# Layers 0 and 1 with images held as 4 rows x 32 channels, and three of four sign pieces on GpSimd

## The chip, the cores and the metric

The kernel runs on one core of one Trainium2 chip. A core has five engines that run side by side: TensorE (PE, matmuls and transposes), VectorE (DVE), ScalarE (ACT), GpSimd (POOL) and SyncE (SP, which issues DMAs); ACT issues DMAs too. The metric is device time in microseconds (us). A conclusion needs the profile for where the time goes and the timed runs for how much it is.

## The reference

An input x of 16 images, 224 x 224 pixels, 32 channels, float32, NHWC, passes four residual layers. Each starts with a group normalization of its input (16 groups of 2 channels over a whole image).

```
x = x + L0(gn(x))   # mean over the image -> W, b -> clip(0, 28) -> int dy, dx; the image shifted by (dy, dx), zeros outside
x = x + L1(gn(x))   # sign(gn(x)) convolved 3x3 ('SAME') with the sum of 4 sign weights, plus a bias
x = x + L2(gn(x))   # relu( spectral part + x @ W.T + b )
x = x + L3(gn(x))   # the same with other weights
# spectral part: DCT along columns (32 modes kept), real FFT along rows (32 modes kept),
# a 32 x 32 complex channel mix for each of the 32 x 32 modes, and both transforms back
```

Layer 1 needs only the sign of the normalized image, that is, each value compared with a threshold (m1 in the code), and layer 2 needs the mean and variance of each output image of layer 1 and its 32 x 32 modes.

## The kernel before

It runs five phases one after the other, with a barrier between them. In the names of tensors the first letters tell the phase.

1. Layers 0 and 1 for all images (A_, shift_conv_forward). It writes the output x2s, and for layer 2 the spectrum spec of every image and its mean and variance (statm).
2. The channel mix of layer 2 (MB_, mix_modes).
3. The rest of layer 2 (B_, third_layer): inverse transforms, the 1x1 product, relu, the sum, the forward transform for layer 3. It reads x2s and writes x3s.
4. The channel mix of layer 3 (MC_).
5. The rest of layer 3 (C_, last_layer).

**Layers 0 and 1.** An image in SBUF is a tile of 128 partitions: 4 neighbouring columns x 32 channels; the free dimension runs over the 56 groups of four columns and the 224 rows. Two images are in work at a time, in two buffers. Body(b) of every engine does, interleaved, the convolution of image b, the shift of image b + 1 and the loading of image b + 2, in 9 slots (s = 0 to 8). The tiles of x, 112 rows x 1024 values, arrive by SP's DMAs in the order of use. TensorE transposes each into PSUM (L373, four transposes to a unit of 448 columns, 28 units an image), once for the image as it is (A_aps, copied to the image by ACT with a sum, L525, and squared for the variance, L536), and once for the image shifted by (dy, dx), which is loaded again from other addresses (A_sps, masked where it is outside and added to the image by VectorE, L738 to L749). VectorE makes the signs in four pieces of 14 column groups (L773 to L781): one compare to bf16, a full copy, and two copies of 32 partitions, so that there are two sign tensors (signa, signb). With these the 3x3 convolution of a unit of 448 columns is 6 matmuls of 128 rows x 64 columns of the array (L415), in pairs that use its two halves. VectorE adds the result to the image (L755). ACT squares it (L577). TensorE transposes the result back (L426), ACT copies it (L547) and stores it to x2s in NHWC order; the same copies are the input of the forward row transform (L440, ACT L560). The column transform of an image (the function spectrum: turn_spec L452, ACT's copy L568 into one of two colpart buffers, forward_cols L461) is done in eight rounds during slots 0 and 1 of the next body. Statistics of an image are a chain of short instructions that goes VectorE, TensorE, VectorE, ACT, VectorE, TensorE, VectorE (L683 to L728); between images the order is: last shifted unit, center, centered (L761 to L767, the threshold m1), signs, statistics.

**Layer 2 (third_layer).** An image is 4 rows x 32 channels: partition 32 i + c holds channel c of the rows 4 l + i, l = 0 to 55. Since x2s is NHWC, each image is loaded in eight chunks of eight DMAs (L1168) and turned by 16 VectorE transposes of 32 x 32 blocks (turn_in, L1347). Then, for 14 units (e) of 896 columns: TensorE's 1x1 product (L1253) and inverse column transform (L1263), VectorE's relu and sum (L1377), ACT's squares (L1307) and store. The forward transform of image b - 1 stands between them: VectorE transposes it (turn_out, L1370), TensorE transforms (L1225, L1235), VectorE turns the results (L1357, L1364). The image is loaded and turned in units e = 6 to 13 of the image before; TensorE waits at the start of an image until all 16 transposes are done.

The order of all work is written out by hand in these bodies; loops over images repeat them. Each engine executes its instructions strictly in order, and all else is semaphores.

## Time and profile before

| | us |
|---|---|
| median of 3 timed runs | 3808.79 (3801.92 to 3814.15) |
| the profiled execution's own time | 3800.75 |
| its span, first to last instruction | 3798.7 |
| layers 0 and 1 (first convolution added at 172.1, last at 1792.1) | about 0 to 1816 |
| channel mix of layer 2 | about 1819 to 1950 |
| layer 2 (first product at 1991.8, last transposes at 3070.2) | about 1951 to 3090 |
| channel mix of layer 3 and layer 3 | about 3090 to 3798.7 |

| engine | busy us | share of the span |
|---|---|---|
| PE | 2990.2 | 79% |
| PE weight loads | 1622.4 | 43% |
| DVE | 2738.1 | 72% |
| ACT | 1522.8 | 40% |
| POOL | 36.9 | 1% |

Busy shares are means over phases with different limits, so they are read by phase. A matmul's end is modelled, so what a group of matmuls costs is read from the distance between starts. The granted clock is the TensorE clock in parts of 2.4 GHz.

### The profile page before, as it was taken

What the parts mean: (1) busy time and instruction counts of PE and PEld (TensorE: products, weight loads), DVE (VectorE), ACT (ScalarE), POOL (GpSimd) and SP (SyncE); (2) the same over time, 40 slices, a digit from 0 to 9 for tenths busy, and PEclk for the clock granted to TensorE, in tenths of its full rate; (3) what the DMA queues carried; (4) which work ended last, traced back from release to release, by engine and by line L of the source; (5) the groups of instructions that cost most, each with busy time, mean ns of one, the idle gap of its engine ahead of it and who ended that gap; (6) DMA issues with size and microseconds to landing.
All of it is one profiled execution on the core that took longest, in us unless ns stands there. A gap on an engine that the chain in (4) does not pass through costs nothing. (4 is left out here: it accounts for less than half of the span.)

```text
span 3798.7 us, 64095 instructions
## 1 busy us (share of the span) xinstructions
PE 2990.2 (79%) x20528; PEld 1622.4 (43%) x20528; DVE 2738.1 (72%) x4615; ACT 1522.8 (40%) x3060; POOL 36.9 (1%) x23
## 2 busy tenths in 40 slices
PE   2688888888888888888348787887878735999997
PEld 2455555555554555544243333333333315444443
DVE  2566666666566666665537889989898744899998
ACT  3477766666677766655312222222222213000000
POOL 0000000000000000000100000000000010000000
PEclk9799998999899998989658899898898965999998
DMA  4566765666666675653657757767576353999998
GB/s 121 160 196 191 207 203 169 183 177 187 173 194 177 199 207 169 184 163 110 137 150 222 234 196 224 219 213 226 191 243 192 141 120 103 345 387 386 383 386 296
DMA packets 244496, 793.86 MB, mean 209 GB/s; under 512 B 41706, under 2 KB 76190, under 8 KB 233396
## 3 DMA queue, kind: packets, MB, share of 16 engines
q1 hardware_dynamic: 172692, 473.01, 42.4%
q10 hardware_dynamic: 70912, 316.72, 23.7%
q8 instruction: 143, 2.34, 0.3%
q14 instruction: 141, 1.16, 0.1%
q0 software_dynamic: 608, 0.63, 0.1%
HBM read 464.31 MB, written 329.10 MB: 209 GB/s over the span
## 5 line engine op out<-in xcount | busy, mean ns | idle before, releaser
L1307 ACT ACTIVATE B_junk<-B_im,B_nk 128x896 bf16<-128x896 f32 x224 | 233.4, 1042 | 855.9 <-DVE B_im L1377 659.0
L1253 PE MATMUL B_ring<-B_im,B_wnorm 128*128 128x448 f32 x896 | 413.3, 605 | 157.7 <-DVE B_im L1347 155.9
L755 DVE SCALAR_TENSOR_TENSOR A_image<-A_cps,A_cbias,A_image 128x448 f32<-128x448 f32 x448 | 303.3, 681 | 226.8 <-PE A_cps L415 200.8
L1576 PE MATMUL C_ring<-C_im,C_wnorm 128*128 128x448 f32 x896 | 387.8, 571 | 24.4 <-DVE C_ubuf L1633 19.0
L415 PE MATMUL A_cps<-A_signa,A_cwa 128*64 128x448 bf16 x1344 | 354.1, 378 | 63.9 <-DVE A_signa L781 43.0
L373 PE MATMUL A_aps<-a_k_ident,A_tin 112*128 112x112 f32 x1792 | 274.8, 297 | 108.2 <-ACT A_image L525 72.3
L415 PE MATMUL A_cps<-A_signb,A_cwb 128*64 128x448 bf16 x1344 | 354.8, 378 | 0.0
L547 ACT ACTIVATE A_tout<-A_aps 112x512 f32<-112x512 f32 x448 | 242.4, 591 | 266.4 <-PE A_aps L426 266.1
L1253 PEld LDWEIGHTS B_ring<-B_im,B_wnorm 128*128 128x128 f32 x896 | 172.9, 204 | 402.7 <-issue 334.5
L1225 PE MATMUL B_ring<-B_rout,iB_k_rowf 128*64 128x512 f32 x896 | 269.3, 684 | 76.4 <-DVE B_rout L1370 76.1
L749 DVE SCALAR_TENSOR_TENSOR A_image<-A_sps,A_lin,A_image 128x448 f32<-128x448 f32 x448 | 304.4, 682 | 13.4 <-PE A_sps L373 3.2
L525 ACT ACTIVATE A_image<-A_aps 128x448 f32<-128x448 f32 x448 | 240.3, 541 | 166.3 <-PE A_aps L373 161.9
L373 PE MATMUL A_sps<-a_k_ident,A_tin 112*128 112x112 f32 x1792 | 275.7, 280 | 39.6 <-DVE A_image L749 19.8
L1377 DVE SCALAR_TENSOR_TENSOR B_im<-B_ring,B_im 128x896 f32<-128x896 f32 x224 | 239.5, 1071 | 82.1 <-PE B_ring L1263 80.1
L1347 DVE STREAM_TRANSPOSE B_im<-B_rin 128x896 f32<-128x896 f32 x256 | 284.1, 1110 | 14.8 <-DMA B_rin<-x2s 10.3
L373 PEld LDWEIGHTS A_aps<-a_k_ident,A_tin 112*128 112x128 f32 x1792 | 205.2, 158 | 177.0 <-ACT A_image L525 71.0
L373 PEld LDWEIGHTS A_sps<-a_k_ident,A_tin 112*128 112x128 f32 x1792 | 184.1, 146 | 200.1 <-issue 148.5
L1642 DVE STREAM_TRANSPOSE C_rout<-C_im 128x2048 f32<-128x2048 f32 (+1 forms) x128 | 259.4, 2028 | 5.9 <-DMA out<-C_rout 4.0
L1370 DVE STREAM_TRANSPOSE B_rout<-B_im 128x2048 f32<-128x2048 f32 (+1 forms) x128 | 256.3, 2023 | 0.0
L426 PE MATMUL A_aps<-a_k_ident,A_image 128*112 128x128 f32 x1792 | 240.9, 278 | 18.1 <-ACT A_tout L547 18.1
L1576 PEld LDWEIGHTS C_ring<-C_im,C_wnorm 128*128 128x128 f32 x896 | 159.1, 189 | 216.2 <-issue 163.1
L1648 DVE SCALAR_TENSOR_TENSOR C_im<-C_ring,C_im 128x896 f32<-128x896 f32 x224 | 234.9, 1069 | 14.7 <-PE C_ring L1586 12.7
(195 smaller groups left out, 4023.9 us busy)
## 6 DMA issues: line engine op xcount, KB each, us to landing
A_tin<-in_x SPq DMA_DIRECT2D x441, 448.0 KB, 4.9
B_rin<-x2s SPq DMA_DIRECT2D x1024, 112.0 KB, 3.4
x2s<-A_tout ACTq DMA_DIRECT2D x224, 448.0 KB, 4.4
x3s<-B_im ACTq DMA_DIRECT2D x112, 896.0 KB, 5.0
C_im<-x3s SPq DMA_DIRECT2D x112, 896.0 KB, 13.0
out<-C_rout ACTq DMA_DIRECT2D x192, 256.0 KB
out<-C_rout ACTq DMA_DIRECT2D x192, 192.0 KB
out<-C_rout ACTq DMA_DIRECT2D x64, 128.0 KB
```

Of the source, the lines that this page charges most:

```text
L373: last = nc.tensor.transpose(dst[:, j * HR:(j + 1) * HR], src[:, (4 * s + j) * P:(4 * s + j + 1) * P], con["k_ident"][0:HR, 0:HR])
L415: last = nc.tensor.matmul(cps[n % 2][64 * g:64 * g + 64, 0:2 * SIZE], wts[:, tap, :], src[:, j0:j0 + 2, 1 + tap:1 + tap + SIZE], start=(ta ...
L426: last = nc.tensor.transpose(aps[v % 2][0:HR, j * P:(j + 1) * P], image[par][:, j0 + j, half * HR:(half + 1) * HR], con["k_ident"][:])
L547: nc.scalar.activation(tout[u % OUTS][:, v % 2, :], aps[v % 2][0:HR, :], ACT.Copy).then_inc(a_copied, 1)
L749: nc.vector.scalar_tensor_tensor(out=dst, in0=t[:, :, :], scalar=lin[par][:, 0:1], in1=dst, op0=ALU.mult, op1=ALU.add, accum_out=addsum[:, ...
L755: nc.vector.scalar_tensor_tensor(out=dst, in0=cps[n % 2][:, 0:2 * SIZE].rearrange("p (j r) -> p j r", r=SIZE), scalar=cbias[par][:], in1=d ...
L1225: last = nc.tensor.matmul(bank[64 * side:64 * side + 64, hq, :], con["k_rowf"][:, t, :], rout[p % 2][:, t, q0:q0 + BANK], start=(t == 0), ...
L1253: nc.tensor.matmul(slot(par, ("add", e))[:, lane % 2, 0:2 * SIZE], wnorm[par][:], im[par][:, EVN * e:EVN * (e + 1)].rearrange("p (m s) -> ...
L1347: nc.vector.transpose(turned_view(im[par], j0, ch * CHQ, CHQ), flat_view(rin[slot][:, t, :])).then_inc(turned_in, 1)
L1370: nc.vector.transpose(flat_view(rout[p % 2][:, t, 0:wide * C]), turned_view(im[par], j0, p * PAIRQ, wide)).then_inc(rout_full, 1)
L1576: nc.tensor.matmul(slot(add_place(e))[:, lane % 2, 0:2 * SIZE], wnorm[par][:], im[par][:, EVN * e:EVN * (e + 1)].rearrange("p (m s) -> p s ...
L1642: nc.vector.transpose(flat_view(rout[p][:, 0:wide * C]), turned_view(im[par], SECOND * t, p * PIECEQ, wide)).then_inc(rout_full, 1)
```

## The change

Layers 0 and 1 get the layout that layer 2 has: 4 rows x 32 channels. From this follow all other parts.

- **Loading.** x comes in 16 tiles of 28 columns (CHQ) an image, four DMAs of 32 partitions each, and again for the shifted image. TensorE no longer transposes them: VectorE does, with 32 x 32 block transposes, straight into the image (turn_x), or into a tile `moved` that it masks and adds (add_shifted). Three image buffers take the place of two. ACT sums and squares the tiles from SBUF (x_tile).
- **Bodies of 16 slots** with 14 convolution units of 896 columns; two tables, X_BY and S_BY, say how many tiles of either kind are done by the end of each slot.
- **Convolution.** For each unit, 6 matmuls of the whole 128 x 128 array (rows inside the groups of four) and 12 of 32 x 32 (from the neighbouring group, with every second element read and written), in place of 2 x 6 matmuls of 128 x 64 in the kernel before.
- **Signs.** A single sign form, no shifted copies. Piece 0 (8 row pairs of 448 values) is made by VectorE; pieces 1, 2 and 3 (9, 9 and 8 of 448) by GpSimd, into two buffers used in turn: piece 1 as soon as piece 0 is done, piece 2 after 4 units of the convolution, piece 3 after 7.
- **Forward transform.** Columns first, then rows. The first part has half the matmuls (L507); the second has, in each of eight rounds, a copy into one colpart buffer (before: two) and four matmuls of 128 columns with 64 x 64 weights.
- **Outputs.** x2s is stored straight from the image, in the image's own layout. The spectrum is stored in 8 DMAs whose runs in DRAM are 32 values (before: one DMA with rows of 512 values).
- **Layer 2** loads x2s in 7 DMAs an image into the image buffer; its rin buffers, chunks and turn_in are gone. It loads image b + 1 when image b - 1 has been turned out, squared and stored.

The mixes and layer 3 are unchanged.

```diff
-        image = [sb(f"image{i}", [P, NBLK, SIZE]) for i in range(2)]
-        signa = sb("signa", [P, NBLK * RP], bf16)
-        signb = sb("signb", [P, NBLK * RP], bf16)
-        tin = [sb(f"tin{i}", [HR, TW]) for i in range(RING)]
+        image = [sb(f"image{i}", [P, NPIX]) for i in range(3)]
+        sign = [sb(f"sign{i}", [P, (CHL + 2) * LPW + 8], bf16) for i in range(2)]
+        rin = [sb(f"rin{i}", [P, CHQ * C]) for i in range(RING)]
+        moved = sb("moved", [P, TN])
...
-        colpart = [sb(f"colpart{i}", [HR, BANK]) for i in range(2)]
+        colpart = sb("colpart", [64, BANK])
...
+        X_BY = [0, 2, 5, 7, 9, 11, 13, 14, 15, 16, 16, 16, 16, 16, 16, 16]
+        S_BY = [0, 0, 0, 1, 2, 3, 4, 6, 8, 10, 13, 16, 16, 16, 16, 16]
...
             def store_spec(b):
                 sp.wait_ge(spec_sb, b + 1)
-                sp.dma_start(spec[bass.ds(b, 1)].rearrange("o p m -> (o p) m"), specout).then_inc(spec_stored, 16)
...
+                planes = plane.rearrange("(g e c) (m y) -> g e m c y", g=4, e=2, m=16)
+                for e in range(2):
+                    for g in range(4):
+                        sp.dma_start(planes[g, e],
+                                     specout[64 * e + 16 * g:64 * e + 16 * g + 16, :].rearrange("m (c y) -> m c y", y=MODES)
+                                     ).then_inc(spec_stored, 16)
...
             def conv(b, n):
...
-                for tap in range(3):
-                    for g, (src, wts) in enumerate(((sa, cwa), (sbb, cwb))):
-                        last = nc.tensor.matmul(cps[n % 2][64 * g:64 * g + 64, 0:2 * SIZE], wts[:, tap, :],
-                                                src[:, j0:j0 + 2, 1 + tap:1 + tap + SIZE],
-                                                start=(tap == 0), stop=(tap == 2), skip_group_check=True)
...
+                def edges(u_top, u_bottom):
+                    for tap in range(3):
+                        nc.tensor.matmul(banks[bottom, u_top, 0:LPN].rearrange("p (j s) -> p s j", s=2), cedge[top, tap, :],
+                                         above(2 * n + u_top, tap), start=False, stop=False, skip_group_check=True)
+                        nc.tensor.matmul(banks[top, u_bottom, 0:LPN].rearrange("p (j s) -> p s j", s=2), cedge[bottom, tap, :],
+                                         below(2 * n + u_bottom, tap), start=False, stop=False,
+                                         skip_group_check=True)
...
+                whole(0, 0)
+                whole(1, 0)
+                edges(0, 1)
+                whole(0, 1)
+                whole(1, 1)
+                edges(1, 0)
+                whole(0, 2)
+                whole(1, 2).then_inc(conv_full, 1)
...
+            def add_shifted(b, q, k, at_tile):
...
+                nc.vector.transpose(moved[:, :].rearrange("p (l q s) -> p q l s", q=CHQ, s=2),
+                                    flat_view(rin[at_tile % RING][:, :])).then_inc(tile_turned, 1)
...
+                nc.vector.scalar_tensor_tensor(out=dst, in0=m[:, lo:16, :], scalar=lin[:, 0:1], in1=dst, op0=ALU.mult,
+                                               op1=ALU.add, accum_out=addsum[:, k:k + 1]).then_inc(shift_added, 1)
...
         @block.gpsimd
...
+            def signs(b, q, c):
+                if c == 1:
+                    pool.wait_ge(sign_full, b + 1)
+                    if not isinstance(b, int) or b > 0:
+                        pool.wait_ge(conv_full, UNITS * b)
+                else:
+                    pool.wait_ge(conv_full, UNITS * b + (4 if c == 2 else CHL))
...
+                nc.gpsimd.tensor_scalar(rows[:, lo - CHL * c + 1:hi - CHL * c + 1, 2:2 + LPN], lps(q)[:, lo:hi, :], m1[:], 2.0,
+                                        ALU.is_ge, ALU.mult).then_inc(sign_rest, 1)
...
# third_layer
-            def turn_in(b, par, ch):
...
+            def load(b, par, k):
+                cols = slice(2 * EVN * k, 2 * EVN * (k + 1))
+                sp.dma_start(im[par][:, cols], src[bass.ds(b, 1)].rearrange("o p m -> (o p) m")[:, cols]).then_inc(in_full[par][k], 16)
```

**The order on VectorE inside an image.** Before, in the middle of a body: A_cps holds convolution units of 448 columns, A_sps shifted units; REGISTER_ALU rows count the loop's semaphores.

```order
L753 REGISTER_ALU
L755 SCALAR_TENSOR_TENSOR A_image0,A_convsum0<-A_cps0,A_cbias0,A_image0 128x448 [waits A_conv_full]
L733 REGISTER_ALU
L738 SCALAR_TENSOR_TENSOR A_sps0<-A_sps0,A_nmean1,A_rmask1 128x4x28 [waits A_shift_full]
L644 REGISTER_ALU
L749 SCALAR_TENSOR_TENSOR A_image1,A_addsum<-A_sps0,A_lin1,A_image1 128x4x112 [waits A_step]
```

The changed kernel at the like place (slot 5 of a body):

```order
L826 SCALAR_TENSOR_TENSOR A_image1,A_convsum1<-A_cps1,A_cbias1,A_image1 128x896 [waits A_conv_full]
L886 REGISTER_ALU
L795 STREAM_TRANSPOSE A_image0<-A_rin1 128x28x16x2 [waits A_in_full1,A_junk_done]
L803 REGISTER_ALU
L805 STREAM_TRANSPOSE A_moved<-A_rin2 128x28x16x2 [waits A_in_full2,A_shift_added]
L807 REGISTER_ALU
L817 SCALAR_TENSOR_TENSOR A_moved<-A_moved,A_nmean,A_rmask 128x224 [waits A_tile_turned]
L704 REGISTER_ALU
L820 SCALAR_TENSOR_TENSOR A_image2,A_addsum<-A_moved,A_lin,A_image2 128x16x56 [waits A_step]
```

A unit has twice the columns; the transposes are VectorE's, and the sum of the shifted tile reads two operands from SBUF (moved and the image), where it read one from PSUM (A_sps).

**The order on TensorE at the start of a body**, between two convolution units, where the second part of the transform of the image before stands. Before:

```order
L461 MATMUL A_vps<-A_colpart0,a_k_dctf 32x64 [waits A_a_copied]
L461 MATMUL A_vps<-A_colpart0,a_k_dctf 32x64 x7
L452 MATMUL A_aps0<-a_k_ident,A_rowspec 112x128 [waits A_a_copied]
L452 MATMUL A_aps0<-a_k_ident,A_rowspec 112x128 x3
```

The changed kernel, the end of four rounds and the convolution unit 1 behind them:

```order
L524 REGISTER_ALU
L529 MATMUL A_vps<-A_colpart,a_k_fwdr 64x128 [waits A_a_copied]
L529 MATMUL A_vps<-A_colpart,a_k_fwdr 64x128 x3
L524 REGISTER_ALU
L529 MATMUL A_vps<-A_colpart,a_k_fwdr 64x128 [waits A_a_copied]
L529 MATMUL A_vps<-A_colpart,a_k_fwdr 64x128 x3
L466 MATMUL A_cps1<-A_sign0,A_cfull 128x448 [waits A_conv_added,A_sign_full]
L466 MATMUL A_cps1<-A_sign0,A_cfull 128x448
```

A round's matmuls read the one buffer colpart, which ACT may fill again only when they are done; VectorE's convolution unit 1 stands behind four such rounds, unit 2 behind four more.

**GpSimd's queue in the loop**, empty before:

```order
L934 ISA [waits A_sign_full]
L944 TENSOR_SCALAR A_sign<-A_image,A_m 128x9x448 [waits A_conv_full]
L936 REGISTER_ALU
L944 TENSOR_SCALAR A_sign<-A_image,A_m 128x9x448 [waits A_conv_full]
L936 REGISTER_ALU
L941 MEMSET A_sign 128x448 [waits A_conv_full]
L942 ISA
L944 TENSOR_SCALAR A_sign<-A_image,A_m 128x8x448 [waits A_pool_step]
```

The three compares of an image, each 3584 or 4032 values to a partition.

## Rows read from the trace of the kernel before

**Rows 1.** Windows: span of layers 0 and 1, and one image of layer 2.

```profile
core 0: us, PE busy (x) PEld busy (x) DVE busy (x) ACT busy (x) POOL busy (x), PEclk, DMA share, GB/s
172.10:1792.10 1620.00, 1379.43 (x11115) 838.74 (x11116) 1059.69 (x2894) 1094.32 (x2336) 0.00 (x0) 0.92 0.62 181
2307.50:2374.70 67.20, 54.85 (x248) 21.92 (x248) 59.62 (x68) 15.89 (x28) 0.00 (x0) 0.88 0.64 203
```

**Rows 2.** One line: threshold of each image (ns min/median/max, first to last start).

```profile
L766 DVE COPY A_m<-A_mps x16: 157/159/160, 162.7 to 1730.9; 128x1 f32<-128x1 f32 x16
```

**Rows 3.** One line: after unit 0 of each image in layer 2.

```profile
L1382 DVE TENSOR_SCALAR B_nk<-B_sums x16: 153/154/155, 1999.7 to 2982.9; 128x1 f32<-128x1 f32 x16
```

**Rows 4.** Waits, 300 to 1700 us: total us, times, longest.

```profile
DVE A_image L755 <- PE A_cps L415: 167.1, 59, 5.7
```

**Rows 5.** Timeline of DVE, layers 0 and 1 (start us, us, instruction).

```profile
97.83 0.18 DVE L684 TENSOR_REDUCE A_sm<-A_xsum 128x1 f32<-128x28 f32 x1 [37.07 <-ACT A_xjunk L536]
...
105.46 0.22 DVE L728 TENSOR_SCALAR A_cmask<-a_k_cols,A_sm 128x7 f32<-128x7 f32 x1
...
640.38 0.68 DVE L749 SCALAR_TENSOR_TENSOR A_image<-A_sps,A_lin,A_image 128x448 f32<-128x448 f32 x1
...
641.00 0.68 DVE L755 SCALAR_TENSOR_TENSOR A_image<-A_cps,A_cbias,A_image 128x448 f32<-128x448 f32 x1
```

**Rows 6.** Timeline of PE, layers 0 and 1, with two convolution pairs.

```profile
599.32 0.58 PE L415 MATMUL A_cps<-A_signa,A_cwa 128*64 128x448 bf16 x1
...
635.86 0.35 PE L415 MATMUL A_cps<-A_signa,A_cwa 128*64 128x448 bf16 x1
...
636.05 0.35 PE L415 MATMUL A_cps<-A_signa,A_cwa 128*64 128x448 bf16 x1
...
638.00 1.04 PE L426 MATMUL A_aps<-a_k_ident,A_image 128*112 128x128 f32 x8
...
645.47 1.94 PE L440 MATMUL A_vps<-A_tout,a_k_fwd 112*64 112x512 f32 x8
```

**Rows 7.** Timeline of ACT: a copy of the second transform, a square.

```profile
609.41 0.60 ACT L568 ACTIVATE A_colpart<-A_aps 112x512 f32<-112x512 f32 x1 [0.38 <-PE A_aps L452]
...
623.86 1.03 ACT L577 ACTIVATE A_junk<-A_image,A_nk 128x896 bf16<-128x896 f32 x1
```

**Rows 8.** Groups by line (busy us, mean ns): VectorE's compare.

```profile
L773 DVE TENSOR_SCALAR A_signa<-A_image,A_m 128x3136 bf16<-128x3136 f32 x64 | 118.3, 1848 | 0.5
```

**Rows 9.** One line: GpSimd's long instruction, a memset.

```profile
L929 POOL MEMSET MB_moving<- x1: 6915/6915/6915, 1832.2 to 1832.2; 64x8192 f32 x1
```

**Rows 10.** SP's issues: a plain one, and one of 1024 runs of 512 bytes.

```profile
3.58 0.43 SPq L126 DMA_DIRECT2D a_k_rows<-k_rows  x1
...
1850.30 2.72 SPq L911 DMA_DIRECT2D MB_wmode<-in_L_conv_R_real  x1
```

**Rows 11.** DMA issues: count, KB each, median us to landing.

```profile
B_rin<-x2s SPq DMA_DIRECT2D x1024, 112.0 KB, 3.4
```

**Rows 12.** Timeline of DVE in one image of layer 2.

```profile
2309.05 4.45 DVE L1370 STREAM_TRANSPOSE B_rout<-B_im 128x2048 f32<-128x2048 f32 x2
...
2343.47 1.09 DVE L1377 SCALAR_TENSOR_TENSOR B_im<-B_ring,B_im 128x896 f32<-128x896 f32 x1 [2.29 <-PE B_ring L1263]
...
2344.68 2.25 DVE L1347 STREAM_TRANSPOSE B_im<-B_rin 128x896 f32<-128x896 f32 x2
2346.86 1.05 DVE L1377 SCALAR_TENSOR_TENSOR B_im<-B_ring,B_im 128x896 f32<-128x896 f32 x1
```

**Rows 13.** Timeline of PE in the same image.

```profile
2307.50 4.99 PE L1253 MATMUL B_ring<-B_im,B_wnorm 128*128 128x448 f32 x8 [8.22 <-DVE B_im L1347]
...
2332.84 6.27 PE L1225 MATMUL B_ring<-B_rout,iB_k_rowf 128*64 128x512 f32 x16 [3.41 <-DVE B_rout L1370]
...
2343.36 3.65 PE L1225 MATMUL B_ring<-B_rout,iB_k_rowf 128*64 128x512 f32 x8
...
2351.96 3.80 PE L1235 MATMUL B_ring<-B_gbuf,iB_k_colf 128*64 128x512 f32 x16 [0.64 <-DVE B_gbuf L1357]
2355.70 3.41 PE L1253 MATMUL B_ring<-B_im,B_wnorm 128*128 128x448 f32 x8
...
2360.01 1.13 PE L1214 MATMUL B_ring<-B_vbuf,iB_k_invs 64*128 64x512 f32 x4
```

More of the change, by code:

```diff
@@ L229, in shift_conv_forward @@
         spec_stored = sem("spec_stored")
-        stored = [sem(f"stored{i}") for i in range(OUTS)]
+        stored = [sem(f"stored{i}") for i in range(3)]
         mean_in = sem("mean_in")
@@ L506, in _ @@
[L506 to L513 removed]
+                    if has_s and s == 12:
+                        statistics(b, 4)
```

925 lines of the change are left out of this document (468 added, 457 removed).

## The prediction

> **What bounds the kernel now.** I read the windows of the two changed phases first [rows 1]: in layers 0 and 1 TensorE is busy 85% of the time at a granted clock of 0.92, VectorE 65%, ScalarE 68%, GpSimd nothing; in the image of layer 2 VectorE has 89%, TensorE 82%. The threshold comes every (1730.9 - 162.7)/15 = 104.5 us [rows 2], layer 2's first unit every 65.5 us [rows 3]. In the waits, VectorE's convolution sum waits for TensorE 167 us over 59 times [rows 4]: layers 0 and 1 are bound by TensorE, with VectorE in its shadow in most places. In layer 2 the two go in lockstep in the first half of an image, and TensorE starts the image 8.22 us late behind VectorE's transposes of the input [rows 13].
>
> **The change, layers 0 and 1, per image.** TensorE loses all transposes of the input, so VectorE becomes the long engine. Its costs: a transpose of 896 values 1.09 us (two starts 2.18 us apart), a sum of 896 about 1.0 [rows 12]; a sum of 672 values by the same rate 0.8.
>
> - Slots 2 to 11: 10 convolution sums x 1.0, 14 transposes of x tiles x 1.09 = 15.3, 16 of shifted tiles = 17.4, the sums of the shifted tiles 8 x 1.0 + 8 x 0.8 = 14.4, masks 4.8 (one of 896, one of 672 and nine of 224 values, each with a wait for its own end: 1.0 + 0.8 + 9 x 0.33), the image's statistics 1.9 (nine tiny instructions, by the chain in [rows 5]). Together 63.8 us, VectorE without a pause. TensorE has here per slot a convolution unit, one transposing back and half a column transform. A pair of two concurrent half-array matmuls starts 0.19 us after the one before, eight transposes take 1.04 us [rows 6]. With the twelve 32 x 32 matmuls in pairs, a unit is 6 x 0.19 + 6 x 0.19 + 0.2 = 2.5 us, a slot 4.1: hidden behind VectorE's 6.4.
> - Seam, slots 12 to 15, where VectorE waits for TensorE in turn: sum 12 1.0, center 0.3, TensorE's average and unit 13 (behind GpSimd's last piece) 3.4, sum 13 1.0, centered 0.3, sign piece 0 2.6 (3584 values by the compare's 1848 ns for 3136 = 2.1 [rows 8], and a memset), then the chain of statistics 105.46 + 0.22 - 97.83 = 7.85 [rows 5] and 1.6 for its two more mask copies and its hops behind TensorE's queue. 18.1 us.
> - Start of a body, convolution 0's end to sum 2. Before, eight rounds used two colpart buffers; now one. A round is ScalarE's copy 0.6 [rows 7], four matmuls, and two hops of 0.2, one after the other. The matmuls of 128 columns cost between 0.52 (at the 0.13 of a transpose) and 1.04 (twice it, since a chain that starts anew each time is short and alone); I take 1.04, so 2.04 a round, and with the first four transposes 0.5 four rounds are 8.7. So 8.7 + unit 1 2.5 + turn back 1.1 + 8.7 + unit 2 2.5 + 0.2 = 23.7 us, in which VectorE has little to do.
> - Sum 105.6, and 2 for a half clock after TensorE's waits (a convolution matmul is 0.58 us at half clock against 0.35 [rows 6]): 107.5 us.
>
> ScalarE loses the copies of the transposed x, gains squares from SBUF (896 values, 1.03 us [rows 7]); I get 79 us an image, 38 of them in slots 2 to 6 beside VectorE's 37: close, not bounding.
>
> **GpSimd's pieces.** The trace of before has no compare on it, only a memset: 6915 ns for 8192 values [rows 9]. At that rate a piece of 4032 values is 3.4 us; two such passes (one read, one write) 6.8, three 10.2. I take 6. Piece 1 runs beside the chain of statistics, piece 2 from unit 4, piece 3 from unit 7. If nothing on VectorE is held, they cost nothing: the convolution that needs one comes several slots later. VectorE's new work, though, is made of instructions with two operands in SBUF (the shifted sums read moved and the image). If those stand still while a piece runs, each piece costs its length less the 1.5 to 2 us that an instruction in flight or of another kind covers: 3 x 4 = 12 us an image. Bounds 0 and 26 (three times 10.2 - 1.7). No row of before has GpSimd and VectorE together, so this is the term with the widest bounds. I take 12, in between, because all of VectorE's long instructions in slots 4 to 8 are transposes and such sums, and VectorE is the long engine there.
>
> By the Trainium skill, "SBUF — State Buffer", section "Who interferes with whom", a VectorE instruction with two inputs in SBUF and a GpSimd instruction that reads SBUF take turns for a whole instruction; by "GPSIMD Engine Reference", section "Performance versus the Vector engine", simple arithmetic there is about half VectorE's rate or less, an estimate of 6.0 to 8.7 us a piece. No row here shows either. By the one rule alone the period is some 12 to 20 us longer than without it; a page that lets one-input compares run near line rate would leave 3.4 us, and 5 us an image.
>
> **The spectrum's store** was one DMA with long rows. Now it is eight with 4096 runs of 128 bytes. An issue of 1024 runs costs SP 2.72 us, a plain one 0.43 [rows 10], so 4 x 2.72 = 11 us of SP's queue in slot 4, where the tiles' loads stand behind it. Four tiles in the ring cover about 8 us; a tile behind them takes its own four issues and a landing like 3.4 us [rows 11]. A stall of 0 to 9 us, I take 4, near the middle since cover and queue are about equal.
>
> **Sum of the phase.** 107.5 + 12 + 4 = 123.5 against 104.5: +19.0, x 15 = +285. Last image (no shifted work, but TensorE alone in its slots and both halves of the spectrum at the end) +18. Start: two fewer big memsets and copies, fewer transposes in the first image, -12.
>
> **Layer 2.** An image was 65.5 us. Its first half, 2309.05 (first turning out) to 2343.47 (the sum behind a wait of 2.29) = 34.4 us, alternates turning out 4.45 us for two, TensorE's rows 6.27, products [rows 12, 13]: unchanged. The second half, 31.1 us, held the 16 transposes of input, 17.4 us of VectorE. Without them TensorE sets it: rows 3.65, a step of products 2360.01 - 2355.70 = 4.31, columns 3.80, 4.31, small inverse 1.06 to 1.13, 4.31 = 21.4, and the sum ahead with its hop 1.3. Period 57.1. The input now comes into the image buffer itself after image b - 1 is turned out and stored, some 26 us ahead of its use; 6.4 MB at the 181 to 203 GB/s of the windows [rows 1] take 32 to 35 us, but the first of seven parts about 5, and the parts are used one after the other. I add 2 for this and the clock: 59, -6.5 x 15 = -97. The start of the phase loses an image's chunks and 16 transposes before the first product, -25. Together -122; bounds -40 (the second half still lockstep, the load late) and -230 (the 8.22 and 3.41 waits go too).
>
> **Total.** 285 + 18 - 12 - 122 = +169 on the profiled execution's 3800.75 (span 3798.7), 3970; the median shown is 8 above that execution, so 3978, rounded to 3975.
>
> **Rivals.**
> A, the other side: the pieces hold nothing and the store is hidden. Period 107.5, 45 + 18 - 12 - 122 = -71: 3737. The sign turns where the period is 104.5 + 116/15 = 112.2, that is where GpSimd and store together cost under 4.7 us an image. For it: the pieces start several slots early, GpSimd was idle [rows 1], the ring has cover. Against: VectorE has no slack left in slots 2 to 11.
> B, slow pieces: 10.2 us each and held all the while, 25.5 instead of 12, so a period of 137: 15 x 32.5 - 116 = +371, 4180. For it only the count of passes; against it, the memset's 0.84 ns a value [rows 9].
> C, the 32 x 32 matmuls don't run in pairs: a unit is 18 x 0.19 + 0.2 = 3.6, 1.1 more. In slots 2 to 11 that stays hidden (5.2 of 6.4 us), but units 1, 2, 12 and 13 stand on the path: +4.4, period 128, 15 x 23.5 - 116 = +236, 4045. For it: they read and write every second element, a thing that no row shows.
> By the Trainium skill, "DMA: Bandwidth & Descriptors", section "Specifications", pieces under 512 bytes miss the line rate, so the runs of 128 bytes would also land late; no row here shows such a run, and only the next image's last turn waits for it.
>
> **Chances.** The forecast 0.44, A 0.28, B 0.14, C 0.14. B's upper part alone is outside 3730 to 4150. Within 0.3% (11 us, what a measurement can tell) 0.05, between A and the forecast; faster 0.27, slower 0.68. If A or its neighbours hold, the faster end lies near 3730; both signs have weight, so the forecast's own range stands beside: 3880 to 4070.
>
> **What would show it.** Right: the period of the threshold (L837 of the changed kernel) about 123; L944 at about 6 us; shifted sums (L820) much longer than 1.0 us, or the instruction before them stretched, exactly beside a piece; transposes (L795, L805) 1.1; TensorE idle in slots 2 to 11; rounds of the second transform (L520, L626, L529) 2.05 apart; VectorE waiting in slot 4 or 5 for rin with SP's queue in L367; layer 2's period 57 to 59. Wrong: L820 at 1.0 beside L944 (A); L944 over 9 us (B); the starts of L471 and L473 0.19 apart singly, not in pairs (C); a convolution that waits for GpSimd's piece itself; a layer 2 still at 65.

## The result: 19% slower, and the profile after

The changed kernel takes 4538.23 us (median of 4 runs, 4516.48 to 4568.82), the kernel before 3805.36 (4 runs): a ratio of 1.193 (95% interval 1.186 to 1.201). 3975 was predicted and 4180 for the worst rival. The direction was right, the size was not: +733 us for +170.

The profiled execution took 4568.82 us, the longest of the four, with a span of 4567.0; before it was 3798.7, so 768 us are to be found in the profile. Two lines give their places, the threshold of each image and the first unit of each image of layer 2, as in [rows 2, 3] (ns min/median/max, first to last start):

```profile
L837 DVE TENSOR_SCALAR A_m<-A_mps x16: 152/154/158, 166.0 to 2550.4; 128x1 f32<-128x1 f32 x16
...
L1461 DVE TENSOR_SCALAR B_nk<-B_sums x16: 153/154/155, 2849.1 to 3744.4; 128x1 f32<-128x1 f32 x16
```

| | before | after | difference, us |
|---|---|---|---|
| up to the first threshold | 162.7 | 166.0 | +3 |
| 15 images of layers 0 and 1 | 15 x 104.5 | 15 x 159.0 | +816 |
| last threshold to layer 2's first unit | 268.8 | 298.7 | +30 |
| 15 images of layer 2 | 15 x 65.5 | 15 x 59.7 | -88 |
| the rest | 815.8 | 822.6 | +7 |

Layer 2 did what was said of it (59 predicted, 59.7 measured). Nearly all of the loss is in the period of layers 0 and 1: 159.0 us, where 123.5 was expected. It is a mean of fifteen intervals; the first is 132.3 us, the last 150.0, and those between are 157 to 164.

What GpSimd's line says is already outside every bound of the prediction. Below it stand GpSimd's timeline and VectorE's in one image, with piece 1 of the next image at the end (start us, us, instruction):

```profile
L944 POOL TENSOR_SCALAR A_sign<-A_image,A_m x48: 12344/13838/13840, 169.2 to 2620.7; 128x4032 bf16<-128x4032 f32 x32, 128x3584 bf16<-128x3584 f32 x16
```

```profile
1336.81 13.84 POOL L944 TENSOR_SCALAR A_sign<-A_image,A_m 128x4032 bf16<-128x4032 f32 x1 [53.03 <-PE A_cps L466]
...
1365.31 12.35 POOL L944 TENSOR_SCALAR A_sign<-A_image,A_m 128x3584 bf16<-128x3584 f32 x1 [0.20 <-POOL A_sign L941]
1434.12 13.84 POOL L944 TENSOR_SCALAR A_sign<-A_image,A_m 128x4032 bf16<-128x4032 f32 x1 [56.47 <-DVE A_sign L844]
```

```profile
1298.89 1.15 DVE L826 SCALAR_TENSOR_TENSOR A_image<-A_cps,A_cbias,A_image 128x896 f32<-128x896 f32 x1 [7.25 <-PE A_cps L466]
...
1318.26 1.15 DVE L826 SCALAR_TENSOR_TENSOR A_image<-A_cps,A_cbias,A_image 128x896 f32<-128x896 f32 x1 [18.21 <-PE A_cps L466]
...
1331.96 1.15 DVE L826 SCALAR_TENSOR_TENSOR A_image<-A_cps,A_cbias,A_image 128x896 f32<-128x896 f32 x1 [10.52 <-PE A_cps L466]
...
1338.73 9.50 DVE L857 TENSOR_TENSOR A_sm<-A_sm 128x1 f32<-128x1 f32 x1
...
1369.94 6.64 DVE L817 SCALAR_TENSOR_TENSOR A_moved<-A_moved,A_nmean,A_rmask 128x224 f32<-128x224 f32 x1
...
1429.82 1.15 DVE L826 SCALAR_TENSOR_TENSOR A_image<-A_cps,A_cbias,A_image 128x896 f32<-128x896 f32 x1 [7.92 <-PE A_cps L466]
...
1434.47 11.07 DVE L747 TENSOR_TENSOR A_sm<-A_sm 128x1 f32<-128x1 f32 x1
```

A multiplication of one value to a partition (L747) takes 11.07 us; alone it takes 0.16. A masking (L817) of 0.45 us takes 6.64. These three begin while a piece of GpSimd runs, and what they take beyond their own time is 10.9 + 9.3 + 6.2 = 26.4 us in this image. The same lines are held in nearly every image, L817 by 4.7 to 9.4 us. The transposes of 896 values in the same stretches keep their 1.1 us. The four convolution sums (L826) show another thing: VectorE stands 7.25, 18.21, 10.52 and 7.92 us for units 0, 1, 2 and 13 of TensorE.

TensorE shows why. Its timeline at the start of that body, first after the stall of the chain, then 20 us later, and at the end unit 0 of the next body:

```profile
1281.67 0.59 PE L424 MATMUL A_mps<-A_mv,a_k_pair 128*128 128x1 f32 x2 [11.87 <-DVEq L750]
...
1293.02 1.02 PE L471 MATMUL A_cps<-A_sign,A_cedge 32*32 32x448 bf16 x1
...
1293.76 1.02 PE L471 MATMUL A_cps<-A_sign,A_cedge 32*32 32x448 bf16 x1
...
1298.64 1.92 PE L520 MATMUL A_aps<-a_k_ident,A_rowspec 128*64 128x128 f32 x8
...
1310.88 0.93 PE L466 MATMUL A_cps<-A_sign,A_cfull 128*128 128x448 bf16 x2
...
1318.02 1.71 PE L493 MATMUL A_aps<-a_k_ident,A_image 128*112 128x128 f32 x8
...
1327.94 0.55 PE L466 MATMUL A_cps<-A_sign,A_cfull 128*128 128x448 bf16 x2
...
1328.77 0.57 PE L471 MATMUL A_cps<-A_sign,A_cedge 32*32 32x448 bf16 x1
...
1329.15 0.57 PE L471 MATMUL A_cps<-A_sign,A_cedge 32*32 32x448 bf16 x1
...
1331.76 1.04 PE L493 MATMUL A_aps<-a_k_ident,A_image 128*112 128x128 f32 x8
...
1453.04 0.55 PE L466 MATMUL A_cps<-A_sign,A_cfull 128*128 128x448 bf16 x2
...
1456.86 1.04 PE L520 MATMUL A_aps<-a_k_ident,A_rowspec 128*64 128x128 f32 x8
```

A convolution unit is 1331.76 - 1327.94 = 3.8 us at full clock and 7.1 at half clock (1310.88 to 1318.02), four rounds of the second transform 8.0 and 12.2. An edge matmul starts 0.38 us after the one before it on its side at full clock, 0.74 at half. A pair of 128 x 64 matmuls of as many columns took 0.19 [rows 6]. The L473 matmuls stand beside the L471 ones within 0.01 us, so they do run in pairs: the pair itself is slow.

The windows give the granted clock (PEclk), 0.92 before [rows 1]. The stretches are many images, the start of the body, slots 2 to 11, the seam's wait for unit 13, and the chain of statistics:

```profile
core 0: us, PE busy (x) PEld busy (x) DVE busy (x) ACT busy (x) POOL busy (x), PEclk, DMA share, GB/s
400.00:2400.00 2000.00, 1531.30 (x6496) 589.42 (x6498) 1318.04 (x1798) 889.31 (x1687) 494.22 (x49) 0.74 0.45 135
...
1299.60:1332.00 32.40, 29.91 (x140) 16.80 (x139) 3.67 (x7) 8.99 (x16) 0.00 (x0) 0.69 0.10 29
1332.00:1421.70 89.70, 68.54 (x308) 23.91 (x306) 82.27 (x102) 54.14 (x107) 26.66 (x3) 0.81 0.71 209
1421.70:1433.70 12.00, 11.69 (x36) 3.00 (x36) 3.97 (x9) 0.21 (x1) 0.00 (x0) 0.57 0.27 78
1433.70:1447.00 13.30, 1.26 (x8) 1.15 (x7) 12.00 (x8) 2.38 (x5) 12.88 (x1) 0.69 0.00 0
```

In every one of these stalls of some 12 us the clock falls to half while TensorE idles; when it comes back differs. In the body shown it is at half clock, but for 3.4 us before unit 0, until about 1319. Behind the next stall, of 12.04 us, unit 0 runs at full clock (1453.04 to 1456.86, 3.8 us), as it does in 5 of the 14 bodies between the first and the last; from the end of the chain to sum 2 these take 33.5 us, the others 37.7 to 40.5 (35.7 once). Unit 13 runs at half clock in all 14.

### The profile page after: what moved, and what is told of

It is laid out like the page before. It is cut to its first block and busy times, and to the rows that moved or that the text cites. A ratio compares the mean times of both kernels' runs of the same rounds, so it can differ in the third digit from the quotient of the medians.

```text
span 4567.0 us, 58488 instructions
## 1 busy us (share of the span) xinstructions
PE 3492.9 (76%) x17264; PEld 1475.1 (32%) x17264; DVE 3045.1 (67%) x3640; ACT 1493.5 (33%) x2708; POOL 684.9 (15%) x87
## 5 line engine op out<-in xcount | busy, mean ns | idle before, releaser
L944 POOL TENSOR_SCALAR A_sign<-A_image,A_m 128x4032 bf16<-128x4032 f32 (+1 forms) x48 | 640.3, 13340 | 1770.6 <-DVE A_sign L844 993.1
L471 PE MATMUL A_cps<-A_sign,A_cedge 32*32 32x448 bf16 x1344 | 737.5, 695 | 0.0
L473 PE MATMUL A_cps<-A_sign,A_cedge 32*32 32x448 bf16 x1344 | 737.3, 695 | 0.0
L826 DVE SCALAR_TENSOR_TENSOR A_image<-A_cps,A_cbias,A_image 128x896 f32<-128x896 f32 x224 | 257.2, 1149 | 698.0 <-PE A_cps L466 698.0
L466 PE MATMUL A_cps<-A_sign,A_cfull 128*128 128x448 bf16 x1344 | 454.0, 427 | 8.1 <-issue 8.1
L507 PE MATMUL A_vps<-A_tout,a_k_dctj 112*32 112x512 f32 x896 | 294.4, 792 | 133.5 <-ACT A_tout L606 133.2
L493 PEld LDWEIGHTS A_aps<-a_k_ident,A_image 128*112 128x112 f32 x1792 | 279.7, 196 | 241.8 <-issue 196.4
L795 DVE STREAM_TRANSPOSE A_image<-A_rin 128x896 f32<-128x896 f32 x256 | 274.5, 1097 | 84.3 <-DMA A_rin<-in_x 83.3
L805 DVE STREAM_TRANSPOSE A_moved<-A_rin 128x896 f32<-128x896 f32 x256 | 281.4, 1099 | 34.5 <-DMA A_rin<-in_x 25.6
L820 DVE SCALAR_TENSOR_TENSOR A_image<-A_moved,A_lin,A_image 128x896 f32<-128x896 f32 (+1 forms) x256 | 265.0, 1035 | 9.1
L590 ACT ACTIVATE A_junk<-A_image,A_nx 128x896 bf16<-128x896 f32 (+1 forms) x256 | 242.9, 949 | 8.5
## 6 DMA issues: line engine op xcount, KB each, us to landing
C_im<-x3s SPq DMA_DIRECT2D x112, 896.0 KB, 12.2
```

The costliest lines, as they stand in the source:

```text
L466: return nc.tensor.matmul(banks[:, u, 0:LPN], cfull[:, tap, :], straight(2 * n + u, tap), start=(tap == 0), stop=(tap == 2), skip_group_ch ...
L471: nc.tensor.matmul(banks[bottom, u_top, 0:LPN].rearrange("p (j s) -> p s j", s=2), cedge[top, tap, :], above(2 * n + u_top, tap), start=Fa ...
L473: nc.tensor.matmul(banks[top, u_bottom, 0:LPN].rearrange("p (j s) -> p s j", s=2), cedge[bottom, tap, :], below(2 * n + u_bottom, tap), st ...
L493: last = nc.tensor.transpose(aps[half][0:HR, l * P:(l + 1) * P], image[q][:, first:first + 2 * HR].rearrange("p (j s) -> p s j", s=2)[:, l ...
L507: last = nc.tensor.matmul(vps[32 * g:32 * g + 32, :], con["k_dctj"][:, half, :], tout[G % OUTS][:, half, :], start=(half == 0), stop=(half ...
L795: nc.vector.transpose(turned_view(image[q], SECOND * t, ch * CHQ, CHQ), flat_view(rin[slot][:, :])).then_inc(tile_turned, 1)
```

## Experiments

Three questions: is it GpSimd's piece that holds VectorE, and by what rule; why is the edge pair twice as slow; and what is left when both are gone. Ratios are to the kernel before, 95% intervals in brackets. "Period" is that of the threshold in layers 0 and 1, (last start - first start)/15.

### All four sign pieces on VectorE

```diff
+                    if has_v and s == 0:
+                        more_signs(q, 1)
                     if has_v and s < UNITS:
                         add_conv(b, q, s)
+                    if has_v and s in (3, 6):
+                        more_signs(q, 2 if s == 3 else 3)
...
# GpSimd
-                for c in (1, 2, 3):
-                    signs(b, q, c)
```

> All four sign pieces on VectorE: piece 1 ahead of convolution sum 0, pieces 2 and 3 behind sums 3 and 6. Theory (GpSimd's compare holds VectorE's instructions with two operands in SBUF): the holds of 10.9 us (L747), 9.3 us (L857) and 6.2 us (L817) an image go, three compares of about 2.3 us come, of which the first lies where VectorE waits for TensorE; net 26.4 - 4.6 = 22 us an image, 15 x 22 = 330, and some more where TensorE's half clock came from its waits for held instructions: period of the threshold 159 to about 130 to 137, time 4140 to 4230. Rival (the time is TensorE's: the 32x32 matmuls and the half clock, and the held instructions stand where VectorE would have waited anyway): the period stays above 150, time above 4400.

4202.6 us, 1.105 (1.102 to 1.108); period (2210.1 - 166.1)/15 = 136.3. The main theory's number. L747 takes 0.16 us again. The compares of 4032 values came out dearer than expected, two thirds of the 48:

```profile
L852 DVE TENSOR_SCALAR A_sign<-A_image,A_m x48: 2085/4410/4415, 177.4 to 2282.6; 128x4032 bf16<-128x4032 f32 x32, 128x3584 bf16<-128x3584 f32 x16
```

4.41 us for nine row pairs, 2.09 for eight. So GpSimd's part in the loss is about 23 us of period and 336 us of time, even with 10.9 us of compares put on VectorE instead. The other 400 us remain while GpSimd has nothing to do here.

### The chain's two-operand instructions written with one

```diff
-                    link(nc.vector.tensor_tensor(sm[:, 29:30], sm[:, 28:29], sm[:, 28:29], ALU.mult))
+                    link(nc.vector.tensor_scalar(sm[:, 29:30], sm[:, 28:29], sm[:, 28:29], None, ALU.mult))
...                                   # and eleven more of this kind
```

> GpSimd keeps its pieces; the tiny VectorE instructions of the two statistics chains that had two operands in SBUF are written as tensor_scalar with the second operand as a scalar pointer. Theory (the hold goes by the form of VectorE's instruction): the first chain is 10 to 11 us shorter, with no instruction of it over 0.3 us, though the whole of it now lies beside piece 1; the hold beside piece 2 moves from L857 to the next two-operand instruction, the masking of the first shifted tile, at about 8 us; net -11 an image, -165 in all, time about 4370. Rival (any VectorE instruction that starts beside GpSimd's compare is held, or it is the semaphore wait behind it): another instruction of the chain takes the 11 us and the time is unchanged.

4402.1 us, 1.159 (1.154 to 1.164), where 4370 was expected; period (2417.4 - 166.9)/15 = 150.0. GpSimd's piece 1 began at 1212.45 here, piece 2 at 1271.55. VectorE's timeline beside piece 1 and then beside piece 2:

```profile
1212.79 0.21 DVE L747 TENSOR_SCALAR A_sm<-A_sm 128x1 f32<-128x1 f32 x1
1213.04 0.21 DVE L748 TENSOR_SCALAR A_mv<-A_sm 128x1 f32<-128x1 f32 x1
...
1214.46 0.28 DVE L755 TENSOR_SCALAR A_sm<-A_sm,A_mv 128x1 f32<-128x1 f32 x1
...
1218.57 7.74 DVE L766 TENSOR_SCALAR A_wsc<-A_w0s,A_sm 32x2 f32<-32x2 f32 x1
```

```profile
1278.37 5.53 DVE L809 SCALAR_TENSOR_TENSOR A_moved<-A_moved,A_nmean,A_cmask 128x896 f32<-128x896 f32 x1
```

All rewritten instructions up to there run freely beside the piece, so the form decides, as the theory says. The hold beside piece 2 moved to the masking L809 as expected, at 5.53 us and not 8. But the chain was not 10 us shorter: a one-input instruction was held, L766, the first with two values to a partition and its input in SBUF. It ended at 1226.31, when piece 1 ended (1212.45 + 13.84 = 1226.29). The "no instruction over 0.3 us" of the expectation failed on it.

This is where a rule is worth having. The Trainium skill, "SBUF — State Buffer", section "Who interferes with whom", names both: an instruction with two inputs in SBUF contends with a GpSimd instruction that reads SBUF, and one-input copies and tensor_scalar contend too where they run in a two-port mode. These rows agree in kind. For the time the measurement decides: if the end of a held instruction less its own time is taken as the moment when it was let go, the two-input ones (L747, L857, L809) were let go 11.2 to 11.3 us after the piece's start, of 13.84, not at its end. L766 ended within 0.02 us of the piece, so the end of GpSimd's row seems real; what the piece does in its last 2.6 us, and whether L766 runs in such a mode, no run shows.

### GpSimd's three pieces in three forms

```diff
+                if c == 1:
+                    last = nc.gpsimd.tensor_scalar(where, what, m1[:], None, ALU.is_ge)
+                elif c == 2:
+                    last = nc.gpsimd.tensor_scalar(where, what, m1[:], 2.0, ALU.is_ge, ALU.mult)
+                else:
+                    last = nc.gpsimd.tensor_copy(where, what)
```

> GpSimd's three pieces in three forms of the same size per value: piece 1 with one operation (is_ge alone, so the factor 2 is left out of its signs), piece 2 as it was, piece 3 a plain copy to bf16 in place of the compare. If the time goes by operations, piece 1 is well under 13.8 us for 4032 values (about 3.4 us a pass less), and piece 3 is shorter still for its 3584; if it goes by elements whatever the operation, piece 1 stays at 13.8 and piece 3 at 12.3. The holds on VectorE follow the pieces' lengths.

GpSimd's timeline and the hold beside its piece 1:

```profile
1241.26 10.46 POOL L946 TENSOR_SCALAR A_sign<-A_image,A_m 128x4032 bf16<-128x4032 f32 x1 [63.92 <-DVE A_sign L844]
1313.38 13.85 POOL L948 TENSOR_SCALAR A_sign<-A_image,A_m 128x4032 bf16<-128x4032 f32 x1 [61.67 <-PE A_cps L466]
...
1341.40 3.17 POOL L950 CAST A_sign<-A_image 128x3584 bf16<-128x3584 f32 x1 [0.17 <-POOL A_sign L941]
```

```profile
1241.85 8.26 DVE L747 TENSOR_TENSOR A_sm<-A_sm 128x1 f32<-128x1 f32 x1
```

The time goes up with the operations, not in equal steps: 0.88 ns a value for a copy, 2.59 for a compare, 3.43 for a compare and a multiplication. My base, the memset's 0.84 ns [rows 9], is near the price of the copy. The hold shortens with the piece. Time 4484.6 us in its one run.

### Edge matmuls that read or write contiguous values

```diff
+                def put(rows, u):
+                    if n % 4 in (2, 3):
+                        return banks[rows, u, 0:LPN].rearrange("p (s j) -> p s j", s=2)
+                    return banks[rows, u, 0:LPN].rearrange("p (j s) -> p s j", s=2)
...                                   # take(): contiguous reads where n % 4 in (1, 3)
```

> On the kernel with all signs on VectorE; the 32x32 edge matmuls of units 1, 5, 9, 13 read contiguous values, those of units 2, 6, 10 write contiguous values, those of units 3, 7, 11 do both, units 0, 4, 8, 12 are as they were (the values of the edges are wrong in the others). A pair of them starts 0.37 us after the one before at full clock, a pair of 128x64 matmuls of 448 columns in the kernel before 0.19. If reading every second element costs, units 1, 3 fall to about 0.19 a pair; if writing every second column does, units 2, 3; if it is the 32x32 tiles themselves (two at a time in corners that are not beside each other), all stay at 0.37.

Starts of TensorE in unit 5 (contiguous reads), then in unit 6 (contiguous writes), at full clock:

```profile
1277.25 0.58 PE L482 MATMUL A_cps<-A_sign,A_cedge 32*32 32x448 bf16 x1
...
1277.63 0.58 PE L482 MATMUL A_cps<-A_sign,A_cedge 32*32 32x448 bf16 x1
...
1286.05 0.36 PE L482 MATMUL A_cps<-A_sign,A_cedge 32*32 32x448 bf16 x1
...
1286.25 0.35 PE L482 MATMUL A_cps<-A_sign,A_cedge 32*32 32x448 bf16 x1
```

0.38 us apart when only the reads are contiguous, 0.20 when only the writes are. Units 2, 3, 6, 7, 10, 11 had the short pair at full clock, the others the long one (0.36 to 0.38), and with both contiguous (3, 7, 11) it was no shorter, 0.19 to 0.20. So it is the write into every second column of PSUM that costs double; the stepped read costs nothing, and 32 x 32 tiles are not slow. 4118.7 us in one run.

### Rows of a pair in banks of their own

The unit is laid out in PSUM as layer 2 has it: bank s holds the rows of parity s, each matmul writes 448 neighbouring columns and reads with a step of two.

```diff
-                        nc.tensor.matmul(banks[bottom, u_top, 0:LPN].rearrange("p (j s) -> p s j", s=2), cedge[top, tap, :],
...
+                            nc.tensor.matmul(banks[bottom, s_top, cols], cedge[top, tap, :], up,
+                                             start=False, stop=False, skip_group_check=True)
...
-                dst = image[q][:, 2 * LPN * n:2 * LPN * (n + 1)].rearrange("p (l f) -> p l f", f=LPN)
+                dst = image[q][:, 2 * LPN * n:2 * LPN * (n + 1)].rearrange("p (m s) -> p s m", s=2)
```

> All signs on VectorE, and a unit of the convolution laid out in PSUM with the two rows of a pair in a bank each (as layer 2 has it), so that every matmul writes neighbouring columns; reads step by two. Theory (a 32x32 matmul that writes every second column costs double, as the units that wrote contiguously in the last run had 0.20 us a pair against 0.37): a unit takes 2.7 us at full clock instead of 3.8, 5 instead of 6.9 at half clock; units 0, 1, 2 and 13 stand on the path and some of the others where the clock is half, so 5 to 8 us an image, 4080 to 4130. Rival (the whole 128x128 matmuls, which now step by two in their reads, get slower by as much, or TensorE's units are hidden): 4190 to 4210.

In this kernel and the next, the sums of units 3 and 10 leave out a part; their matmuls are all there, and the time is read as it is. 4069.6 us, 1.070 (1.068 to 1.072), a little better than expected; period (2092.2 - 166.4)/15 = 128.4. The edge pairs start 0.20 us apart (1205.82, 1206.01 and 1206.02), and the whole 128 x 128 matmuls, which now read with a step, are no slower (0.20 apart at full clock in both kernels). 7.9 us of period for the writes, 133 us by the medians.

### The order of work

```diff
-        X_BY = [0, 2, 5, 7, 9, 11, 13, 14, 15, 16, 16, 16, 16, 16, 16, 16]
-        S_BY = [0, 0, 0, 1, 2, 3, 4, 6, 8, 10, 13, 16, 16, 16, 16, 16]
+        X_BY = [2, 4, 5, 6, 7, 8, 10, 11, 12, 14, 15, 16, 16, 16, 16, 16]
+        S_BY = [0, 3, 4, 5, 6, 7, 8, 10, 11, 12, 13, 14, 16, 16, 16, 16]
# TensorE
-                    if has_s and s == 12:
+                    if has_s and s == 13:        # now right behind conv(b, 13)
                         statistics(b, 4)
...                                   # compares of nine row pairs as eight and one
```

> As the one before, and three things: the tables start both kinds of tiles in slots 0 and 1, where VectorE waited 10 and 15 us (X_BY 2, 4, 5, ...; S_BY 0, 3, 4, ...), TensorE does unit 13 before the average that the threshold needs, and a compare of 9 pairs is cut into 8 and 1 (9 took 4.41 us, 8 took 2.09). Theory (the body's start and the seam were bound by the order of work, not by an engine): VectorE is busy through slots 0 and 1, the seam loses about 6 us, the period falls from about 130 to 100 to 112 us, time 3600 to 3800, at or below the kernel before. Rival (TensorE or the loads of x set the time once VectorE's waits are filled): period above 118, time above 3870.

3797.5 us, 0.998 (0.996 to 0.999), at the upper end of what was expected; period (1829.7 - 164.1)/15 = 111.0, inside it. 17.4 us of period came from three things together, which no run takes apart: the tables, unit 13 ahead of the average, and the cut compares, which take 3.9 us of work off VectorE (2.45 us in place of 4.41, twice).

### GpSimd busy with data of its own

```diff
+            for k in range(144 + 250 + 250):
...
+                if k < 144:
+                    last = nc.gpsimd.tensor_scalar(where, what, 0.5, 2.0, ALU.is_ge, ALU.mult)
+                elif k < 394:
+                    last = nc.gpsimd.memset(pdst[:], 1.0)
+                else:
+                    last = nc.gpsimd.tensor_copy(where, what)
```

> All signs on VectorE, and GpSimd works on data of its own that nobody waits for, from the start of layers 0 and 1: 144 compares of 560 values (f32 to bf16, with the same two operations), then 250 memsets of 560 bf16 values, then 250 copies f32 to bf16. Theory (the hold is between the instructions, no data is needed for it): while the compares run, VectorE's sums with two operands in SBUF and its compares take up to one GpSimd instruction (about 1.9 us) longer, while transposes (1.07) and sums that read PSUM (1.15) do not; beside the memsets none is longer. If the hold came from the pieces' data or semaphores, nothing is longer anywhere. Whether the copies hold is open.

Mixed. VectorE's shifted sum (two operands in SBUF) and convolution sum (one in PSUM) while the compares ran, and the shifted sum again while the copies ran:

```profile
L821 DVE SCALAR_TENSOR_TENSOR A_image<-A_moved,A_lin,A_image x32: 917/1152/1418, 116.5 to 275.4; 128x896 f32<-128x896 f32 x16, 128x672 f32<-128x672 f32 x16
...
L827 DVE SCALAR_TENSOR_TENSOR A_image<-A_cps,A_cbias,A_image x17: 1141/1148/1152, 185.6 to 334.1; 128x896 f32<-128x896 f32 x17
...
L821 DVE SCALAR_TENSOR_TENSOR A_image<-A_moved,A_lin,A_image x25: 917/1418/1422, 497.8 to 696.1; 128x896 f32<-128x896 f32 x15, 128x672 f32<-128x672 f32 x10
```

The sum that reads PSUM never grows. The other does, so no shared data is needed for a hold. But it grows by 0.27 us at most, not by the 1.9 that I allowed, and the tiny instructions by 0.47 at most. The copies hold it too: its median is 1.42 beside them. Beside the memsets no instruction with two operands in SBUF was longer, but the one sign compare of VectorE that fell there took 2.47 us in place of 2.09, so "none is longer" was wrong. A short GpSimd instruction hardly holds anything. That was not expected, and led to the next run. Time 4221.2 us in one run.

### The changed kernel with pieces cut into rows

```diff
-                nc.gpsimd.tensor_scalar(rows[:, lo - CHL * c + 1:hi - CHL * c + 1, 2:2 + LPN], lps(q)[:, lo:hi, :], m1[:], 2.0,
-                                        ALU.is_ge, ALU.mult).then_inc(sign_rest, 1)
+                for l in range(lo, hi):
+                    last = nc.gpsimd.tensor_scalar(rows[:, l - CHL * c + 1, 2:2 + LPN], lps(q)[:, l, :], m1[:], 2.0,
+                                                   ALU.is_ge, ALU.mult)
+                last.then_inc(sign_rest, 1)
```

> The changed kernel with one thing different: each of GpSimd's pieces is issued as 8 or 9 compares of one row pair (448 values) instead of one of 3584 or 4032. Theory (a held VectorE instruction waits out most of the one GpSimd instruction that is under way, 11.3 us of a long one, and at most about 0.5 us beside the private compares of 560 values): no VectorE instruction stands for more than 1.6 us, the three holds of 10.9, 9.3 and 6.2 us go, and the period falls by 15 to 24 us towards that of the kernel with all signs on VectorE, 4200 to 4310. Rival (the hold belongs to GpSimd's work as a whole, so cutting it only spreads it): the held instructions sum to the same 26 us an image, 4500 or more.

4157.9 us, 1.094 (1.091 to 1.097), better than the 4200 to 4310 expected: 380 us, half of the whole loss, from the size of an instruction. GpSimd is busy for longer, not less (753.7 us for what took 640.3 in 48 pieces), and the held lines are nearly free:

```profile
L945 POOL TENSOR_SCALAR A_sign<-A_image,A_m 128x448 bf16<-128x448 f32 x416 | 753.7, 1829 | 1401.7 <-DVE A_sign L844 904.0 <-PE A_cps L466 494.5 <-POOL A_sign L941 3.2
```

```profile
L747 DVE TENSOR_TENSOR A_sm<-A_sm x16: 159/298/313, 92.3 to 2046.4; 128x1 f32<-128x1 f32 x16
...
L857 DVE TENSOR_TENSOR A_sm<-A_sm x16: 159/483/489, 324.1 to 2280.0; 128x1 f32<-128x1 f32 x16
```

Period (2165.3 - 166.4)/15 = 133.3, so 25.7 us less, against the 26.4 us of holds counted above. It is 45 us faster than with all signs on VectorE.

### Two versions that could beat both

> All signs on VectorE, rows in banks of their own (with the first matmul of a bank alone starting its sum), spread tables, unit 13 ahead of the average, and S_BY beginning 2, 4, 5: two shifted tiles go into slot 0, where VectorE stood 8 us for unit 1. The period was 111.0 us without the last. Expected 105 to 110 us, time 3720 to 3790: faster than the kernel before by 0.5 to 2%. If the loads of the shifted tiles, which start only when the shift is known, come too late for slot 0, no gain: 3790 to 3800.

> As the last, but pieces 1 to 3 on GpSimd, one row pair an instruction. VectorE loses 7.4 us of compares an image; if GpSimd's short instructions hold little, the period is 3 to 7 us shorter than with all signs on VectorE (time 3640 to 3740). Rival: the many short holds (about 26 GpSimd instructions of 1.5 us an image) cost VectorE more than the 7.4 us it saves, or piece 1, some 14 us long, is late for unit 3: at or above the time with all signs on VectorE.

```profile
L832 DVE TENSOR_SCALAR A_m<-A_mps x16: 153/155/158, 166.8 to 1808.2; 128x1 f32<-128x1 f32 x16
...
L832 DVE TENSOR_SCALAR A_m<-A_mps x16: 153/155/159, 165.9 to 1807.3; 128x1 f32<-128x1 f32 x16
```

All signs on VectorE (the first line): 3778.5 us, 0.992 (0.990 to 0.995); period 109.4. It beats the kernel before by 0.8%, small but clear of the noise, at the upper end of what was expected. With GpSimd's row pieces (the second line): 3797.2, 0.997 (0.995 to 1.000), period 109.4 in its profile as well. The first one's profiled execution was its longest, 3810.08 us, and the second's 3789.16, so the equal periods don't rank them; the medians do. The 3 to 7 us that I expected of GpSimd did not come, and the rival held: VectorE's busy time from 400 to 1700 us fell from 1013.94 to 968.61, but TensorE then waited for a late piece (waits: total us, times, longest):

```profile
PE A_cps L458 <- POOL A_sign L940: 58.0, 12, 5.0
```

## Why the prediction was wrong, step by step

**What bounds the kernel, and the direction.** Right: VectorE became the long engine in slots 2 to 11, layer 2 gained 5.8 us an image for the 6.5 predicted, GpSimd's pieces held VectorE's two-operand instructions and not its transposes. Which ones it held was not foreseen: none of the 256 shifted sums (L820, at most 1.15 us), but two instructions of one value in the chains of statistics and one masking.

The image shown above runs from one chain's end to the next, 1291.6 to 1455.6, that is 164.0 us (the mean is 159.0), which is 40 more than predicted. By the prediction's own parts:

| part | predicted | measured |
|---|---|---|
| conv 0 behind the chain | 0, hidden | 7.0 |
| start of body to sum 2 | 23.7 | 33.3 |
| slots 2 to 11 without holds | 63.8, and 4 for the store | 67.8, and 5.4 waiting for loads |
| seam without hold | 18.1 | 24.1 |
| half clock | 2 | in the rows above |
| holds | 12 | 26.4 |

The holds are 14.4 of the 40, the start of the body with conv 0 16.6, the seam 6.0. The row pieces bear this out over all images: without the holds the period was 133.3, where the prediction without its 12 would say 111.5.

**The step that failed: "I take 6" us for a piece, with 10.2 as the bound.** It rested on the only GpSimd instruction of the trace, a memset, and on a count of passes. The forms run shows that the price goes up with the operations: 13.84 us for 4032 values, 2.3 times what I took and above the upper bound. The estimate of 6.0 to 8.7 us from the Trainium skill's "GPSIMD Engine Reference", section "Performance versus the Vector engine", was too low as well; here the measurement decides. The step behind it, that a hold costs the piece less 1.5 to 2 us, was near for the first one (10.9 of 13.84) and too high for the others, since free instructions come first. With 13.84 in it the sum would have given 3 x 12 = 36, too much by 10. B, the rival nearest in kind, put 25.5 on the holds, the size measured, but partly by luck: its piece of 10.2 us was too short and its three full holds too long, and the two errors cancel. It priced nothing else and so stopped at 4180.

**The second: "the twelve 32 x 32 matmuls in pairs, a unit is 2.5 us".** They ran in pairs, but a pair took 0.38 us. C said that no row shows a matmul that writes every second element and then priced only the loss of pairing, at about the same cost, 3.6 us for a unit; 3.8 was measured. Its place was right and its mechanism wrong. The Trainium skill, "SBUF — State Buffer", has a note in the section "Door 1: The DMA port swizzle" that "any non-contiguous PSUM access pattern significantly slows down matmuls". The run agrees, 0.38 us against 0.20; I had not weighed it.

**The third: "2 for a half clock".** In the image shown TensorE idles 11.87 us in the held chain, and then runs the whole of unit 0, four rounds and unit 1 at half clock: 12.2 against 8.0 for the rounds, 7.1 against 3.8 for a unit. Likewise unit 13. That is about 4.2 + 3.3 for the start, 3.1 for unit 0 and 3.4 for unit 13. Where unit 0 ran at full clock its 3.1 were not lost, and the half clock fell on other parts of the start. I had taken it for a small extra and not for a factor of nearly two on the parts that stand on the path. How much of it is the hold's doing is not separated: without holds the mean clock of 400 to 2000 us was 0.83 (pieces in rows), against 0.74 with them and 0.92 before.

**The store.** 8 issues took 5.20 us of SP's queue in this image, not 11. The prediction counted 4096 runs; each of the eight DMAs carries 32.0 KB, 256 runs of 128 bytes, so there are 2048, and its own rate of 2.72 us for 1024 runs gives 5.4 (the median of all 128 such issues is 0.45 us, eight of them 3.6). They landed 2.0 us after their issue at the median, the tiles of x after 2.5, so the short runs were not late:

```profile
1355.06 5.20 SPq L367 DMA_DIRECT2D spec<-A_rowspec  x8
```

VectorE waited 5.4 us for loads in the slots behind it, near the 4 taken; since the 4 came from a queue time of 11 us, luck has a part in that.

**Outside the period.** The start of the phase was 3 us longer and not 12 shorter, the stretch from the last threshold to layer 2 30 longer and not 7 shorter, together 52 us off. This was not taken apart.

**A**, the other side: its condition, pieces that hold nothing, was made nearly true by the row pieces, and the period was 133.3, far from the 111.5 of the sum without holds and the 107.5 of A. So A would have been wrong even then, by the second and third steps.

What stays open: why a two-input instruction is let go at 11.3 us of 13.84 (and at 8.7 of 10.46, 10.8 of 12.35) and L766 only at the end; what decides when TensorE's clock comes back after a stall; and the share of the clock in the loss.

## What to carry to other kernels

Before work goes to GpSimd, know its time per value for that very operation, and list which VectorE instructions will start beside it: those with two operands in SBUF, and here one with a single operand of two values, can stand still for most of one GpSimd instruction, however small they are. Cut GpSimd's work into short instructions; here this alone gave back half of a 19% loss. A new layout is to be checked for the columns that each matmul writes, and its time on the path read at either clock level: here the same unit took 3.8 us at full clock and 7.1 at half.

## What the runs showed that I had not expected

- GpSimd, f32 to bf16, 128 partitions: copy 0.88 ns a value, compare 2.59, compare and multiplication 3.43 (1.83 us for 448 values).
- A VectorE instruction of 0.16 us took 11.07 beside a GpSimd compare of 13.84 us, and at most 0.62 beside compares of 1.83 us (L764; L747 at most 0.31).
- A 32 x 32 matmul of 448 columns that writes every second column of PSUM follows the last at 0.38 us at full clock, one that writes neighbouring columns at 0.20; a step of two in what it reads costs nothing.
- VectorE's compare to bf16 takes 4.41 us for 9 x 448 values and 2.09 for 8 x 448; cut into 8 and 1 it takes 2.45.
